# A DLRM tower with a compressed interaction network: VectorE takes over the last partial sum and the rectifying, and the order of GpSimd's and VectorE's side work changes

## The reference, cut to what matters

```python
e = stack([tbl_f[ids[:, f]] for f in range(32)], axis=1)   # (512, 32, 32): batch, field, d
def _cin_forward(x0, filters):                              # two layers, 128 filters each
    prev, outs = x0, []
    for W in filters:
        z = einsum('bhd,bmd->bhmd', x0, prev)
        cur = relu(einsum('bpd,pn->bnd', z.reshape(b, h * m, d), W[0]))
        prev = cur
        outs.append(cur)
    return sum(concatenate(outs, axis=1), axis=-1)          # (512, 256)
h = concatenate([_cin_forward(e, (filter_0, filter_1)), dense_ctx], axis=1)
h = maximum(h @ W_top1 + b_top1, 0.0)
h = maximum(h @ W_top2 + b_top2, 0.0)
y = h @ W_top3
```

## Time and profile before

| | |
|---|---|
| median of 3 runs | 908.58 us (907.87 to 910.68) |
| the profiled execution | 908.48 us, span 906.7 us |
| mean granted TensorE clock | 0.996 |
| busy: PE, DVE, ACT, POOL | 846.9, 748.0, 726.2, 716.1 us |
| DMA | 124.41 MB, mean 137 GB/s |

### The profile page before, as it was taken

How to read it: one execution, slowest core, us unless ns; L and a number is a source line. 1 busy time by engine, 2 the same in 40 slices (tenths; PEclk the granted TensorE clock), 3 DMA queues, 4 the chain that set the end, 5 groups by cost and what they waited for, 6 DMA issues and landing times.

```text
span 906.7 us, 18108 instructions
## 1 busy us (share of the span) xinstructions
PE 846.9 (93%) x3607; PEld 668.3 (74%) x3607; DVE 748.0 (82%) x2363; ACT 726.2 (80%) x2418; POOL 716.1 (79%) x739
## 2 busy tenths in 40 slices
PE   0189999999998999999999999999999999999997
PEld 0167777777786777787777777787777777787873
DVE  4158888898886889888888898888888998888893
ACT  2158888988886898988888888888888898888882
POOL 7777899878887889878888989877777766677761
PEclk9999999999999999999999999999999999999999
DMA  7035676666765666666577565766676665655440
GB/s 191 12 91 134 156 171 150 145 141 136 158 146 142 147 146 149 136 150 146 144 166 165 141 155 114 156 145 142 161 166 144 143 147 127 155 139 144 94 93 1
DMA packets 59774, 124.41 MB, mean 137 GB/s; under 512 B 9377, under 2 KB 18145, under 8 KB 59746
## 3 DMA queue, kind: packets, MB, share of 16 engines
q0 software_dynamic: 22240, 68.17, 40.2%
q1 hardware_dynamic: 37506, 55.96, 19.7%
HBM read 54.99 MB, written 3.05 MB: 64 GB/s over the span
## 4 chain that ended last, share of the span: by engine, by line
PE 60%; DVE 13%; POOL 12%; issue 11%; DMA 1%; ACT 1%; DVEq 1%; SPq 0%; POOLq 0%; ACTq 0%
PE bank L871 49%; DVE acc L765 10%; PE bank L809 9%; POOL rows L344 4%; POOL pair_low L382 2%; POOL half L364 2%; POOL rows_next L397 1%; POOL parts L356 1%; DVE pair L629 1%; PE bank L918 1%; POOL w_sb L366 1%; DVE parts L765 1%; DVE cur_low L640 1%; DMA shifts<-x_scratch 1%; ACT parts L563 0%
## 5 line engine op out<-in xcount | busy, mean ns | idle before, releaser
L563 ACT ACTIVATE parts<-bank,x 128x128 f32<-128x128 f32 x2048 | 591.6, 382 | 118.0 <-PE bank L871 108.6
L765 DVE SCALAR_TENSOR_TENSOR acc<-bank,x,acc 128x128 f32<-128x128 f32 x1792 | 485.3, 342 | 94.2 <-PE bank L871 94.1
L871 PE MATMUL bank<-w_high,cur_high 128*128 128x512 f32 x1024 | 407.5, 398 | 5.7 <-DVE acc L765 3.6
L871 PE MATMUL bank<-w_low,cur_high 128*128 128x512 f32 x1024 | 400.1, 391 | 0.0
L871 PE MATMUL bank<-w_high,cur_low 128*128 128x512 f32 x992 | 388.6, 392 | 0.0
L871 PEld LDWEIGHTS bank<-w_high,cur_high 128*128 128x128 f32 x1024 | 192.5, 188 | 62.3 <-DVE acc L765 19.1
L871 PEld LDWEIGHTS bank<-w_low,cur_high 128*128 128x128 f32 x1024 | 192.6, 188 | 39.4
L871 PEld LDWEIGHTS bank<-w_high,cur_low 128*128 128x128 f32 x992 | 186.5, 188 | 41.2
L364 POOL TENSOR_TENSOR half<-parts 128x512 f32<-128x512 f32 x126 | 165.1, 1310 | 61.5 <-DMA parts<-parts 61.3
L382 POOL TENSOR_TENSOR pair_low<-pair,pair_high 128x512 fp32r<-128x512 f32 x124 | 158.6, 1300 | 28.0 <-ACT pair_high L498 24.0
L397 POOL DMA_INDIRECT rows_next<-table_dram,ids_next x96 | 98.1, 1022 | 30.6 <-issue 30.3
(11 more groups left out here) (90 smaller groups left out, 492.1 us busy)
## 6 DMA issues: line engine op xcount, KB each, us to landing
parts<-parts POOLq DMA_DIRECT2D x126, 512.0 KB, 5.7
shifts<-x_scratch SPq DMA_DIRECT2D x155, 256.0 KB, 3.9
x<-x_scratch SPq DMA_DIRECT2D x31, 256.0 KB, 2.9
x_scratch<-turned SPq DMA_DIRECT2D x31, 64.0 KB
rows_next<-table_dram,ids_next POOLq DMA_INDIRECT x96
wt<-w_top_dram SPq DMA_DIRECT2D x2, 512.0 KB
x_scratch<-turned SPq DMA_DIRECT2D x31, 32.0 KB
rows<-table_dram,ids_sb POOLq DMA_INDIRECT x32, 2.4
```

The lines of the kernel that those rows point to most:

```text
L563: ins = nc.scalar.activation(parts[q][ab][:, at:at + N2], act_bank[ab][:, i * N2:(i + 1) * N2], ACT.Copy, scale=x0[u][:, h, 2 * q + ab:2 * ...
L765: nc.vector.scalar_tensor_tensor(out=dst, in0=dve_bank[e % 2 * 2 + ab][:, i * N2:(i + 1) * N2], scalar=x0[u][:, h, 2 * q + ab:2 * q + ab + ...
L871: return nc.tensor.matmul(dst[:], cur_half[u][:, cols], w1_half[:, fields], **flags)
```

## The change

Three things change. VectorE's product of step 4 and ScalarE's cast of it move one group later. GpSimd's order around its DMAs and gathers changes. And the last two partial sums are added by VectorE straight into PSUM (`dve_total`, slot 20), with the rectifying moved into the addition to the running sum; GpSimd's `sum_left` and ScalarE's `act_total` go. GpSimd now waits for VectorE (`totalled`) before it overwrites `left`.

```diff
-DVE_PAIR = {0: (1,), 4: (2, 0), 8: (3,), 12: (4,)}
+DVE_PAIR = {0: (1,), 4: (2, 0), 8: (3,), 16: (4,)}
-ACT_PAIR_HIGH = {4: 1, 8: 2, 13: 3, 16: 4}
+ACT_PAIR_HIGH = {4: 1, 8: 2, 13: 3, 17: 4}
-ACT_TOTAL, DVE_FOLD = 20, 24
+DVE_TOTAL, DVE_FOLD = 20, 24
...
                 src = parts[t // 2 % 2][t % 2]
+                if t % DC == 0:
+                    pool.wait_ge(totalled, chunk + 1)
...
-            def sum_left(chunk):
-
-                pool.wait_ge(tree, (chunk + 1) * (DC * TREE))
-                pool.wait_ge(total_rectified, chunk + 1)
-                nc.gpsimd.tensor_tensor(total.rearrange("p (t n) -> p t n", t=DC), left[:, :, 0, :], left[:, :, 1, :],
-                                        ALU.add).then_inc(totalled, 1)
...
                     if t % DC == 0 and (next_block or t < tiles - DC):
-                        pair_lows(k * CPB + t // DC + 1, (2, 3))
+                        pair_lows(k * CPB + t // DC + 1, (2,))
                     add_halves(k * (tiles // 2) + t // 2, t // 2 % 2)
+                    if t % DC == 0 and (next_block or t < tiles - DC):
+                        pair_lows(k * CPB + t // DC + 1, (3,))
+                    if t % DC == 2 and (next_block or t < tiles - DC - 2):
+                        pair_lows(k * CPB + t // DC + 2, (0, 1))
                     for s in (t, t + 1):
                         if (next_block and s < rows_at) or (one_after and s > rows_at):
                             for f in late[s]:
                                 gather(f)
-                    if t % DC == 2 and (next_block or t < tiles - DC - 2):
-                        pair_lows(k * CPB + t // DC + 2, (0, 1))
                     for s in (t, t + 1):
                         sum_parts(k * CPB + t // DC, k * (tiles // 2) + t // 2, s)
-                        if s % DC == DC - 1:
-                            sum_left(k * CPB + t // DC)
...
-        def act_total(act, c, pairs_before):
-
-            act.wait_ge(totalled, c + 1)
-            act.wait_ge(paired, pairs_before)
-            nc.scalar.activation(x4_bank[:], total, ACT.Relu).then_inc(total_rectified, 1)
...
+        def dve_total(dve, c):
+
+            dve.wait_ge(tree, (c + 1) * (DC * TREE))
+            nc.vector.tensor_tensor(x4_bank[:].rearrange("p (t n) -> p t n", t=DC), left[:, :, 0, :], left[:, :, 1, :],
+                                    ALU.add).then_inc(totalled, 1)
+
         def dve_fold(dve, c, k):
 
-            dve.wait_ge(total_rectified, c + 2)
-            nc.vector.tensor_tensor(block_sum(k), x4_bank[:], block_sum(k), ALU.add).then_inc(folded, 1)
+            dve.wait_ge(totalled, c + 2)
+            nc.vector.scalar_tensor_tensor(out=block_sum(k), in0=x4_bank[:], scalar=0.0, in1=block_sum(k), op0=ALU.max,
+                                           op1=ALU.add).then_inc(folded, 1)
...
+                            if slot == DVE_TOTAL and not (first and u == 0):
+                                dve_total(dve, c - 1)
```

More of the change, by code:

```diff
@@ L133, in dlrm_tower @@
         left = free[:, 0:DC * 2 * N2].rearrange("p (t l n) -> p t l n", t=DC, l=2)
-        total = free[:, DC * 2 * N2:DC * 3 * N2]
         z2, y_sb = pair[1], pair[0][0:1, 0:B]
@@ L228, in dlrm_tower @@
         totalled = sem("totalled")
+        last_totalled = sem("last_totalled")
         total_rectified = sem("total_rectified")
@@ L443, in _ @@
             pool.wait_ge(tree, (PAIRS - 1) * (2 * TREE))
-            pool.wait_ge(total_rectified, CHUNKS)
             nc.gpsimd.tensor_tensor(first_totals.rearrange("p (t n) -> p t n", t=2), left[:, 0:2, 0, :],
-                                    left[:, 0:2, 1, :], ALU.add).then_inc(totalled, 1)
+                                    left[:, 0:2, 1, :], ALU.add).then_inc(last_totalled, 1)
             pool.wait_ge(folded, CHUNKS - 1)
@@ L451, in _ @@
                                     ALU.add).then_inc(last_tree, 1)
-            pool.wait_ge(total_rectified, CHUNKS + 1)
+            pool.wait_ge(total_rectified, 1)
             pool.wait_ge(last_tree, 1)
@@ L576, in body @@
                                     act_turn(act, c + 2)
-                                if slot == ACT_TOTAL and not (first and u == 0):
-                                    act_total(act, c - 1,
-                                              CHUNKS * STEPS if last and u == UNROLL - 1 else (c + 2) * STEPS)
                                 if slot == ACT_X4 and not last:
@@ L588, in _ @@
             body_loop(act, body)
-            act.wait_ge(totalled, CHUNKS)
+            act.wait_ge(last_totalled, 1)
             act.wait_ge(z1_step, 2)
@@ L673, in _ @@
             nc.vector.memset(sum2[:], 0.0).then_inc(zeroed, 1)
-            nc.vector.memset(acc[:, 0, 0, 0:1], 0.0).then_inc(total_rectified, 1)
+            nc.vector.memset(acc[:, 0, 0, 0:1], 0.0).then_inc(totalled, 1)
             dve.wait_ge(w0_in, 5 * 16)
```

## The result

The changed kernel takes 923.23 us (median of 6 runs, 921.63 to 923.85) against 908.56 us (6 runs): 1.0157 times as long, interval 1.0143 to 1.0171, so 14.7 us slower. The forecast was 931, with 918 to 943 as the range, and slower as the sign. The profiled execution took 923.85 us, span 922.0.

What follows compares the result with a forecast made beforehand. TensorE, busy 93%, was taken to bound the kernel, with GpSimd's `pair_low` of step 3 having 0.57 us in hand. Waits of 16.3 and 6.0 us, 22.3 together, on 908.48 gave 931 us, range 918 to 943.

Steps and rivals of the forecast that it cites:

- Part 1 and 2, the first wait: Gathers behind subtractions, `sum_left` gone: `pair_low` of step 3 is 1.23 us later, TensorE waits 0.66 us; 16.3 us in all.
- Part 3, the second wait: DMAs between subtractions of steps 3 and 4: TensorE waits for step 4, 0.3 us in 20 chunks, 6.0 us.
- A plain chunk: Chunks 1 to 20, with gathers: TensorE's waits for steps 3 and 4 lengthen each by about 1 us.
- the waits of the earlier trace: TensorE's 2.76 and 1.30 us waits for `pair_low`: no margin there, so the whole 1.23 us delay of step 3 counts.
- The clock: TensorE's granted clock falling behind the two longest waits as they grow: 0 to 3.4 us more, left out of the sum.
- Part 4: VectorE's moved product and new addition: about 0.68 us per chunk, hidden in its 2.10 us wait for TensorE; nothing.
- one sign of being right: In the profile after, VectorE's new addition is followed by a wait for TensorE.
- the rival of the first wait only: TensorE waits only for step 3, as step 4's `pair_low` comes in time: 925 us, chance 0.15.
- The contention rival: VectorE's addition falls on a GpSimd operation in every chunk: 12 us more, 943 us, chance 0.12.
- The faster one: Gathers cost nothing behind the subtractions, `pair_low` of step 3 is 1.39 us earlier everywhere: 904 us, chance 0.07.
- the one without change: GpSimd loses 1.4 to 1.9 us from the gathers' move, taken by its 0.57 us margin: 908.5 us, chance 0.04.
- The low end of the range: The 0.30 us gap ahead of each gather hidden behind a tensor operation, 12 us off: 919; range given from 918.

Runs made afterwards that it cites:

- the run with one gather ahead: Changed kernel with one of the two gathers put back ahead of the subtractions of steps 1 and 2: 905.84 us, ratio 0.9977 against the kernel before.
- the run without the second wait: Changed kernel with the subtraction of step 4 put back straight behind that of step 3, ahead of the DMAs: 918.48 us, ratio 1.0110.
- the total alone: Kernel before with only `dve_total` and the rectifying in `dve_fold` added, all orders as before: 903.35 us, ratio 0.9943.

## Why the prediction was right, and where its sizes were off

**Part 1 and 2, the first wait: the mechanism is shown, the size was 0.1 to 0.2 us too large.** The casts, the gathers and the freed operation add up as written: undoing the gathers' move takes the loss away, and GpSimd's 1.39 us are worth 1.33 per chunk (26.6 / 20) when they are put back. Leaving out the loop's turn, TensorE's idle time for step 3 was 0.23 us in the first of these chunks and 0.30 to 0.40 in the others, and there the product came 0.46 to 0.56 us behind its pace, where 0.66 was forecast. Two causes are seen. The gathers, with their gaps, take 2.53 us behind a subtraction (441.93 + 1.28 to 445.74) instead of 2.71, mostly because the first gap is 0.16 and not 0.30. And I took the chunk of the earlier trace rows for all; in every other one the cast of step 2 ends 0.08 us earlier against TensorE's pace (4.75 us ahead of the product of step 1 instead of 4.67), and the product of step 3 is as much less late.

**Part 3, the second wait: right.** `pair_low` of step 4 let the product start 4.62 us behind the start of the one of step 3 (449.89 to 454.51); 4.56 to 4.86 was the range, and 0.27 us per chunk (0.16 and the restart) was measured where 0.3 was taken, in 19 chunks and not in 20: the one at the loop's turn has no second wait. The undoing gave 4.8 us. No gap of 0.30 showed between the DMAs and the subtraction: it ended 1.34 us behind them, close to the 1.28 that one takes alone.

**The terms that failed: the special chunks.** A plain chunk was to grow by 1.07 us and grew by 0.85 in the mean; 16 of these make 3.5 us of the 7.9 by which the sum (22.3) was above the loop's 14.4. The rest lies in four chunks. In two, GpSimd copies the rows of the next block ahead of its DMAs, and TensorE waited there already before; I counted them as plain, but they grew by 0.45 and 0.51 us, since with its DMAs issued earlier GpSimd was no longer behind when the chunk began. The other two are the waits of the earlier trace rows, for which I took 1.53 us each. The chunk at the loop's turn grew by 0.39: GpSimd's idle time there, 3.44 us in the earlier trace rows, was 2.69 in the changed kernel, which leaves 0.48 of the 1.23, and TensorE's wait went from 2.76 to 3.22. The other shrank by 0.62, because what had made it late before is this gap of 1.92 us ahead of a gather. Its cause isn't shown. It stands at the same gather in every kernel here that has both gathers ahead of the subtractions (before, and the three runs with that order), and in none of the others:

```profile
533.87 1.00 POOL L397 DMA_INDIRECT rows_next<-table_dram,ids_next  x1 [1.92 <-issue]
```

I took two one-time waits of before as if they would stay and grow. The clock, left out of the sum with 0 to 3.4 us as its price, added nothing: in the loop it fell once, behind the wait of 3.22 us, to 0.66 in the mean of 5 us, as in the earlier trace rows.

**Part 4: free, as forecast, though not for the reason given.** The addition was to take 0.68 us and hide in an idle time of 2.10. It took up to 2.88, and with the late group before it used up that cover and the extra one from TensorE's own lateness; VectorE's waits for TensorE ahead of `acc` fell from 94.1 to 22.5 us. So one sign of being right failed: in 19 of the 20 chunks with gathers no wait for TensorE follows the addition (452.22 + 2.80 to 454.94); where nothing is gathered one of 0.57 us does. TensorE's waits for `acc` didn't grow. That it costs next to nothing in the end is shown by the run with one gather ahead: the addition took 2.10 us in the mean there, and the time is 905.84, against 904.61 with 1.61 us and 903.35 with 0.71. The Trainium skill's rule ("SBUF — State Buffer", Who interferes with whom), that the blocked one waits for the whole instruction, fits: the addition ended 0.56 us behind the subtraction, nearly its own length. That the one which issues first wins can't be read off the starts of the records: VectorE's addition began at 452.22, GpSimd's subtraction at 452.48, and VectorE waited. The subtraction was queued behind the DMAs then, and its record begins before these end (451.26 + 1.86 = 453.12).

**The rivals.** By the time alone the rival of the first wait only, 925, is nearer to 923.23 than the forecast's 931; the measurement couldn't choose between them. The trace and the run without the second wait (4.8 us less) do: the second wait is there, and both terms were smaller than forecast, part 1 by 0.1 to 0.2 us a chunk. The contention rival had the right resource and the wrong payer: it was VectorE that waited, in idle time. The faster one needed a loss below 1.39 us in part 1 and the one without change 1.4 to 1.9; it was about 2.4. The low end of the range took 0.30 us off for each gather; 0.14 was found, for the first of the two, some 3 us in all.

## What to carry to other kernels

An engine whose queue is in order can be busy 79% of the time and still have half a microsecond in hand: compute for the one handover that the bound engine needs by when it is ready and by when it is wanted, and hold each reordering against that difference. Work that doesn't depend on the awaited engine belongs ahead of the wait, as much of it as the wait is long; one gather of two did nearly all. When a change of three parts is slower, try the parts alone before dropping it: one of them was worth 5.4 us. And where a wait comes once, as at a loop's turn, look at it by itself: here the forecast's two worst terms were such waits, and the gain of the total alone came from such places.

## What the runs showed of the hardware

A VectorE addition with both inputs in SBUF (128x512 fp32, 0.69 us alone) took 2.80 us beside a GpSimd subtraction of the same size, and 0.69 us beside GpSimd's issue of plain DMAs alone. In all 29 chunks of the changed kernel in which it took over 1.3 us it ended 0.56 to 0.58 us behind the end of the subtraction, though it began from 0.34 us before the subtraction's record to 0.91 behind. Beside a small GpSimd operation, whose record began 0.17 us behind its own, it was the other one that paid: with the subtraction of step 4 ahead of the DMAs the addition took 0.76 us and GpSimd's mark of 128x1 took 0.64 instead of 0.19:

```profile
450.12 0.76 DVE L651 TENSOR_TENSOR bank<-w_sb 128x512 f32<-128x512 f32 x1
450.29 0.64 POOL L353 TENSOR_TENSOR mark<-mark 128x1 f32<-128x1 f32 x1
```

What decides who waits is left open. And the second dense layer's 16 matmuls, the same in all the kernels, took 7.13 us in four of the ten profiled executions and 8.81 to 8.98 in the other six; in the changed kernel's the granted clock around them was 0.88, in that of the kernel before 1.00.
